# A graph network kernel: one merged pass for the second graph's rows, and expert tiles gathered by slot lists instead of scattered

## What is computed

```python
x = x + _L0_ffn_ref(_layernorm(x)[None], ...)[0]      # softmax over 64 slices in 8 heads, attention between slices,
                                                      # out_x @ W_out + b_out
x = x + _L1_gnn_ref(_layernorm(x), W_u, b_u, W_v, src, dst)   # per edge: s_u = xn @ W_u.T + b_u, s_v = xn @ W_v.T
# _L1_ffn_ref: a mixture of 8 experts
logits = xt @ Wr + br; probs = softmax(logits)
top_p, top_idx = top_k(probs, 2); weights = top_p / top_p.sum()
xe = layernorm(xt) * ln_g[e] + ln_b[e]
y = gelu(xe @ W1[e] + b1[e]) @ W2[e] + b2[e]
out = sum over the 2 chosen experts of weight * y
```

## Time and profile before

| | us |
|---|---|
| median of 3 runs | 5433.22 (5426.08 to 5433.31) |
| the profiled execution, its own time | 5424.74 |
| its span on the core | 5422.7 |
| mean granted TensorE clock | 0.793 of full |

### The profile page before, as it was taken

One profiled execution on the slowest core, in us unless ns is written; L12 is line 12 of the kernel. 1 busy time (PEld: TensorE's weight loads), 2 busy tenths in 40 slices (PEclk: granted clock), 3 DMA queues, 4 the chain that ended last, 5 costly groups with the idle time before them and its releaser, 6 DMA issues. The chain is left out here.

```text
span 5422.7 us, 84287 instructions
## 1 busy us (share of the span) xinstructions
PE 3370.2 (62%) x13516; PEld 2423.1 (45%) x13517; DVE 2164.5 (40%) x4578; ACT 1770.5 (33%) x6845; POOL 2313.1 (43%) x2387
## 2 busy tenths in 40 slices
PE   4401766666777766598844555545455550599998
PEld 3200443343444444365723333333333340599998
DVE  4401655555656555785523333333233332011111
ACT  2100333333333333242323233333333353344443
POOL 5151545454555555100455555555555535222222
PEclk9855888888888888798767777777777755799999
DMA  8441332233332323320133333333333332566665
GB/s 200 119 120 42 81 74 77 73 75 75 79 79 76 77 75 77 79 62 2 42 80 80 87 80 82 81 82 80 78 83 83 79 110 75 144 181 181 177 181 147
DMA packets 321085, 509.24 MB, mean 94 GB/s; under 512 B 153801, under 2 KB 222442, under 8 KB 320534
## 3 DMA queue, kind: packets, MB, share of 16 engines
q0 software_dynamic: 127744, 324.85, 24.3%
q1 hardware_dynamic: 180523, 179.06, 11.5%
q10 hardware_dynamic: 12770, 4.81, 0.4%
HBM read 429.99 MB, written 79.01 MB: 94 GB/s over the span
## 5 line engine op out<-in xcount | busy, mean ns | idle before, releaser
L822 POOL DMA_INDIRECT g_rows<-rows,g_recs x1856 | 1757.1, 947 | 1700.5 <-DVE g_msg L978 1001.9
L863 PE MATMUL g_pA<-g_msg,k_ident 128*128 128x264 f32 x3712 | 1157.4, 466 | 426.4 <-DVE g_msg L978 350.6
L863 PEld LDWEIGHTS g_pA<-g_msg,k_ident 128*128 128x128 f32 x3712 | 836.7, 236 | 784.6 <-issue 626.7
L978 DVE TENSOR_TENSOR g_msg<-g_rows,g_pp 128x1024 f32 (+1 forms) x464 | 565.4, 1218 | 1224.9 <-ACT g_pp L919 1116.3
L936 ACT ACTIVATE g_accs<-g_pA,g_cs x2928 | 709.5, 304 | 1047.8 <-issue 697.2
L851 PE MATMUL g_pE<-g_ew,g_recT 128*128 128x512 f32 x936 | 617.1, 795 | 424.8 <-ACT g_recT L897 401.4
L865 PE MATMUL g_pA<-g_accs,k_ident 128*128 128x264 f32 x928 | 347.0, 460 | 459.5 <-ACT g_accs L936 350.3
L851 PEld LDWEIGHTS g_pE<-g_ew,g_recT 128*128 128x128 f32 x936 | 211.2, 241 | 652.2 <-issue 631.0
L865 PEld LDWEIGHTS g_pA<-g_accs,k_ident 128*128 128x128 f32 x928 | 197.9, 226 | 546.1 <-ACT g_accs L936 379.7
L1926 POOL DMA_INDIRECT out<-e_ys,e_goal x102 | 157.1, 1540 | 600.6 <-issue 564.8
L1961 PE MATMUL e_pH<-e_xT,e_w 128*128 128x128 f32 x3264 | 384.6, 276 | 0.0
(11 more groups left out here) (394 smaller groups left out, 3521.9 us busy)
## 6 DMA issues: line engine op xcount, KB each, us to landing
e_w<-in_L_ffn_W SPq DMA_DIRECT2D x110, 1024.0 KB
g_rows<-rows,g_recs POOLq DMA_INDIRECT x1856
xs<-f_zero SPq DMA_DIRECT2D x1, 13674.0 KB
e_xs<-xs SPq DMA_DIRECT2D x102, 128.0 KB
g_recs<-slots SPq DMA_DIRECT2D x468, 8.0 KB
rows<-p_row SPq DMA_DIRECT2D x50, 119.0 KB
own<-p_row SPq DMA_DIRECT2D x50, 119.0 KB
p_x<-in_x SPq DMA_DIRECT2D x1, 5600.0 KB
```

The source lines that it names most:

```text
L822: pool.indirect_dma_start(out=rows[:, r, j, :], out_offset=None, in_=rows_d, in_offset=bass.IndirectOffsetOnAxis(ap=recs[:, r, 4 * j:4 * j ...
L863: t_.matmul(pA[:, b, 0:MW], K["ident"][:], msg[:, b, j, :], start=(j == 0), stop=False)
L978: v.tensor_tensor(to, of, by, ALU.mult).then_inc(msg_ok, 1)
```

## The change

**The second graph's rows.** f3 becomes one pass, written out without loops. In slot p TensorE multiplies tile p by `mm`, straight from `swT` (no copies on GpSimd), into one of four PSUM tiles, transposes tile p - 10 and makes the scores of tile p - 11. VectorE adds the product to `x`, takes the statistics, every seventh slot computes mean and variance of the last seven tiles, and two slots later their scales. ScalarE writes the normalized tile directly into the row buffer, which has eight rows of tiles instead of six. The bias is no longer added tile by tile: in f2 one eighth of it is added to every row of `mm` (the slice weights of each of 8 heads sum to one).

**The expert tiles.** Instead of scattering each node's row twice, e0 writes the normalized rows once and in order to a new DRAM tensor `tok`, 7 DMAs of 7 tiles from SyncE, each row with its output row number and both weights; row 0 is the pad. The list of rows for each expert tile is made on the chip: a place in the list is split in its low 7 bits and the tile number; for each of 98 pairs of node tile and choice VectorE makes a one-hot matrix of the low bits (`at_lo`, 128x128) and one of the tile numbers (`at_hi`, 128x106) times a code, twice the row number in `tok` plus 0 or 1 for the choice, and TensorE accumulates all 98 products in one PSUM tile. Its column t is the list of tile t; a place that no node takes stays 0, the pad row. In e1 GpSimd loads a tile's rows by an indirect gather with column t of the list (`load`), where SyncE had a plain DMA. It issues `load` of tile t + 3 between the add of tile t - 1 and that of tile t. VectorE picks output row and weight of a tile from the gathered rows (`keep`), two tiles ahead. The zeroing of `xs` and the strided DMA of the row numbers go away. The diff, cut to its core:

```diff
 KC = HID // 128
-XW = D + 2
...
-            zero = m2.sb("f1_zero", [Q, XW])
-            zeroed = T("zeroed"); z_out = T("z_out")
...
-                    pool.memset(zero[:], 0.0).then_inc(zeroed, 1)
-                    pool.wait_ge(zeroed, 1)
-                    pool.iota(zero[:, D:D + 1], pattern=[[0, 1]], base=N, channel_multiplier=1, allow_small_or_imprecise_dtypes=True).then_inc(zeroed, 1)
...
-                    sp.wait_ge(zeroed, 2)
-                    sp.dma_start(dr["xs"].rearrange("(t p) c -> p t c", p=Q), over(zero[:], 1, MT)).then_inc(z_out, 16)
-                    sp.wait_ge(z_out, 16)
...
+                    sp.dma_start(bout[:], ins["L0_ffn_b_out"].unsqueeze(0).broadcast_to([128, D])).then_inc(b_in, 16)
...
+                    dve.wait_ge(b_in, 16)
+                    ch.link(v.tensor_scalar(bout[:], bout[:], 1.0 / FH, None, ALU.mult))
...
-                    v.tensor_copy(mm[:].rearrange("p (a b) c -> p a (b c)", a=2), pM[:])
+                    v.tensor_tensor(mm[:].rearrange("p (a b) c -> p a b c", a=2), pM[:].rearrange("p a (b c) -> p a b c", b=2),
+                                    over(over(bout[:], 1, 2), 1, 2), ALU.add)
...
+            RB, PB, GT, LAG = 8, 4, 7, 10
...
+                    def product(t):
+                        if t >= PB:
+                            pe.wait_ge(y_used, t - PB + 1)
                         for k in range(4):
-                            last = t_.matmul(pY[b][:], swb[:, b, k, :], mm[:, k, :], start=(k == 0), stop=(k == 3))
+                            last = t_.matmul(pY[t % PB][:, 0:D], swT[:, k, t, :], mm[:, k, :], start=(k == 0), stop=(k == 3))
                         last.then_inc(y_ok, 1)
...
+                    def turn(t):
                         pe.wait_ge(xn_ok, t + 1)
+                        if t >= 2:
+                            pe.wait_ge(xnT_ok, t - 1)
                         for k in range(2):
-                            last = t_.transpose(pT[b][:, k, 0:Q], xn[:, b, k * 128:(k + 1) * 128], K["ident"][0:Q, 0:Q])
+                            last = t_.transpose(pT[t % 2][:, k, 0:Q], row[:, t % RB, k * 128:(k + 1) * 128], K["ident"][:])
                         last.then_inc(t_ok, 1)
...
+                    for p in range(QT + LAG + 1):
+                        if p < QT:
+                            product(p)
+                        if p == LAG:
+                            pe.wait_ge(w_in, 48)
+                        if 0 <= p - LAG < QT:
+                            turn(p - LAG)
+                        if 0 <= p - LAG - 1 < QT:
+                            scores(p - LAG - 1)
...
+                    def root(g):
+                        ts = slice(g * GT, (g + 1) * GT)
+                        act.wait_ge(stats, g + 1)
+                        s.activation(norm.rstd[:, ts], norm.rstd[:, ts], ACT.Sqrt).then_inc(sq, 1)
+                    def normed(t):
+                        act.wait_ge(rst, t // GT + 1)
+                        if t >= RB:
+                            act.wait_ge(row_out[t % RB], 16 * (t // RB))
+                        s.activation(row[:, t % RB, 0:D], x1[:, t, :], ACT.Identity, bias=norm.nbias[:, t:t + 1],
+                                     scale=norm.rstd[:, t:t + 1]).then_inc(xn_ok, 1)
...
+                    root(0)
+                    for t in range(QT + 1):
+                        if t < QT:
+                            if t % GT == GT - 2 and t // GT + 1 < ng:
+                                root(t // GT + 1)
+                            normed(t)
+                        if t >= 1:
+                            turned(t - 1)
...
+                    def update(t):
                         dve.wait_ge(y_ok, t + 1)
-                        dve.sem_inc(pace, 1)
-                        ch.link(v.tensor_tensor(xt, xt, pY[b][:], ALU.add))
...
+                        v.tensor_tensor(x1[:, t, :], x1[:, t, :], pY[t % PB][:, 0:D], ALU.add).then_inc(y_used, 1)
+                        dve.wait_ge(y_used, t + 1)
+                        norm.tile(v, t, x1[:, t:t + 1, :]).then_inc(tile_ok, 1)
...
+                    def ready(t):
+                        dve.wait_ge(u_ok, t + 1)
+                        v.tensor_copy(K["sdst"][:, t, :], pU[t % 2][:, H:2 * H])
+                        v.tensor_tensor(row[:, t % RB, D:RW], pU[t % 2][:, 0:2 * H], bu[:], ALU.add).then_inc(row_ok, 1)
+                    for p in range(last_slot):
+                        g = (p - GT - 2) // GT
+                        if p >= GT + 2 and (p - GT - 2) % GT == 0 and g < ng:
+                            dve.wait_ge(sq, g + 1)
+                            norm.scales(v, ch, rst, slice(g * GT, (g + 1) * GT))
+                        if p < QT:
+                            update(p)
+                            if p % GT == GT - 1:
+                                dve.wait_ge(tile_ok, p + 1)
+                                norm.variance(v, ch, stats, slice(p - GT + 1, p + 1))
+                        if p == LAG:
+                            dve.wait_ge(w_in, 48)
+                        if 0 <= p - LAG - 1 < QT:
+                            ready(p - LAG - 1)
...
+            xall = m2.sb("e0_xall", [Q, QT, XW])
+            xt = xall[:, :, 0:D]
+            xrow = m2.sb("e0_xrow", [Q, 2, D])
...
+                    sp.wait_ge(pad_ok, 2)
+                    sp.dma_start(dr["tok"][0:1, :], pad[:]).then_inc(tok_out, 16)
+                    sp.wait_ge(meta_ok, 1)
+                    kept = dr["tok"][1:1 + NPAD, :].rearrange("(t q) c -> q t c", q=Q)
+                    for g in range(QT // GT):
+                        sp.wait_ge(row_ok, GT * (g + 1))
+                        sp.dma_start(kept[:, g * GT:(g + 1) * GT, :], xall[:, g * GT:(g + 1) * GT, :]).then_inc(tok_out, 16)
+                    sp.wait_ge(tok_out, 16 * (QT // GT + 1))
...
+                    for t in range(QT):
+                        q = QL if t == QT - 1 else Q
+                        for k in range(2):
+                            s = 2 * t + k
+                            pe.wait_ge(at_ok, s + 1)
+                            t_.matmul(pL[:, 0:MT], at_lo[0:q, s % B, :], at_hi[0:q, s % B, :], start=(s == 0), stop=(s == 2 * QT - 1)).then_inc(listed, 1)
...
-                    def row(u, r, first):
...
-                            act.wait_ge(sent[r], 32 * u)
-                            act.sem_inc(pace, 1)
-                        for k in range(2):
-                            last = s.activation(xrow[:, r, k, 0:D], flat(xt[:, tc, :]), ACT.Identity, bias=norm2.nbias[:, tc],
-                                                scale=norm2.rstd[:, tc])
-                        last.then_inc(row_ok, 1)
...
+                    for t in range(QT):
+                        s.activation(xall[:, t, 0:D], xall[:, t, 0:D], ACT.Identity, bias=norm2.nbias[:, t:t + 1],
+                                     scale=norm2.rstd[:, t:t + 1]).then_inc(row_ok, 1)
...
+                        ch.link(v.tensor_scalar(lo_i[:], pos[k][:], Q - 1, None, ALU.bitwise_and))
+                        ch.link(v.tensor_copy(lo[k][:], lo_i[:]))
+                        ch.link(v.tensor_scalar(pos[k][:], pos[k][:], 7, None, ALU.arith_shift_right))
+                        ch.link(v.tensor_copy(hi[k][:], pos[k][:]))
+                    for t in range(QT):
+                        for k in range(2):
+                            s = 2 * t + k
+                            if s >= B:
+                                dve.wait_ge(listed, s - B + 1)
+                            v.tensor_scalar(at_lo[:, s % B, :], iota_q[:], lo[k][:, t:t + 1], None, ALU.is_equal)
+                            v.tensor_scalar(at_hi[:, s % B, :], iota_q[:, 0:MT], hi[k][:, t:t + 1], code[k][:, t:t + 1], ALU.is_equal, ALU.mult).then_inc(at_ok, 1)
...
+                    dve.wait_ge(listed, 2 * QT)
+                    ch.link(v.tensor_copy(code_i[:], pL[:, 0:MT]))
+                    v.tensor_scalar(lst[:], code_i[:], 1, None, ALU.arith_shift_right)
+                    ch.link(v.tensor_scalar(second_i[:], code_i[:], 1, None, ALU.bitwise_and))
+                    ch.link(v.tensor_copy(second[:], second_i[:]))
+                    ch.link(v.tensor_scalar(first_of[:], second[:], -1.0, 1.0, ALU.mult, ALU.add))
...
-                    def scatter(u, r, q):
-                        pool.wait_ge(idx_ok, u * R + (r + 1))
-                        pool.sem_inc(pace, 1)
-                        pool.wait_ge(row_ok, u * R + (r + 1))
-                        pool.sem_inc(pace, 1)
-                        for k in range(2):
-                            pool.indirect_dma_start(out=dr["xs"], out_offset=bass.IndirectOffsetOnAxis(ap=idx[r][k][0:q, 0:1], axis=0),
-                                                    in_=xrow[0:q, r, k, :], in_offset=None).then_inc(sent[r], 16)
...
-                    def load(u, b):
```

(45 more changed lines are left out.)

257 lines of the change are left out of this document (80 added, 177 removed).

## The result

The changed kernel takes 5571.14 us, median of 6 runs (5564.57 to 5573.47); the kernel before, 5429.55 over 6 runs (5419.95 to 5433.31). The ratio is 1.0261, 95% interval 1.0248 to 1.0274: 142 us slower, where 80 us faster was forecast. The profiled execution took 5570.72 us, with a span of 5569.0.

The account below looks back on a forecast made before the run. TensorE was taken to bound the expert tiles (busy 744 of 762 us), while scatters before them left it idle. 5424.7 - 44 - 89 - 6 + 55 = 5341, plus 8.5 for the median: 5350 us, range 5275 to 5430.

Parts of the forecast that it names:

- Merged pass: f3: one pass in TensorE-bound slots of 2.43 us, ending at 2680; gain 44 us, bounds 35 and 50.
- Rival C: f3: the merged pass falls to the half clock, 241 us instead of 132; 5459 us in all; chance 7%.
- Lists: Between routing and expert tiles: 98 one-hot pairs of 0.46 us replace the scatters; gain 89 us, bounds 74 and 104.
- Rival D: One-hot list loop: 1 us a pair if every VectorE-TensorE handshake shows; 53 us more, 5403 us; chance 8%.
- Start: Start of the expert tiles: most of TensorE's 5.76 us wait at tile 2 goes; gain 6 us, bounds 0 and 9.
- Gather in the steady stage: Expert tiles: gather late by 1.1 us, each step 0.55 longer; 99 steps cost 55 us, bounds 15 and 150.
- the ring: Expert tiles: gather of tile t + 3 hangs on tile t - 1's result; two steps a turn, 14.5 + 1.1 us.
- rival B: Expert tiles: gather waits behind a whole W1 load, late by 5.0 us, step 2.5 longer; 5543 us; chance 10%.

Follow-up runs that it names:

- the version whose tiles wait for nothing: Changed kernel with VectorE's small copies moved earlier and the gather of tile t+4 issued ahead of the add of tile t: 4151.8 us.
- no add: Changed kernel with expert rows written to the output without the accumulating add: 4382.7 us.
- half of W1: Changed kernel loading only the first half of W1's columns for all tiles after the first two: 4327.9 us.
- filler: Changed kernel with 10 extra 128x128 identity products on TensorE before the wait for gathered rows of every even tile from tile 4 on: 4391.1 us.

## Why the prediction was wrong, by its own steps

**Merged pass (44 us).** Right in all its parts: slots of 2.40 us for 2.43, clock 0.93 over the stretch, end at 2680.39 + 1.57 = 2682 for 2680, 42 us. On the other chips 35, since the old pass is shorter there. Rival C did not come.

**Lists (89 us).** The loop was right: 42.9 us (4457.4 to 4500.3) for 45; and the block that follows stands at 4505.0, where the working gives 4548.5 - 43.1 = 4505.4. That VectorE sets the pace (0.44) and not TensorE (0.46) was missed and made no difference. The gain was 102, because the old end was mis-sized: I let the expert tiles begin 1.9 us after the last scatter, at 4638, while the row of the next block in the earlier trace rows says 4650.48, 14.5 us after that scatter's end. What fills those 14.5 us is not shown: the DMA engines move nothing from 4642 on. Rival D did not come.

**Start (6 us).** The first activation comes 2.9 us later after its block (9.0 against 6.1: the first gather lands in 5.5 us, behind two W1 loads), and the wait at tile 2 is gone. The runs with and without it, 734.9 and 724.5 us, give 10.4, all in the first steps, since later both take 7.25 us a step: net 7.5.

**Gather in the steady stage (55 us).** Its working holds where no weights are in front: copy and semaphores from the add's end to the gather's start 1.0 us (1.2 taken with the gap), landing 2.06 (1.86). With W1 moved behind, the stage is 67 us longer than before; since that includes the faster start, the ring itself costs 77 for 55, 1.5 us a pair for 1.1. The step that failed is another: the landing was priced with nothing in front of the gather, 1.86 us, and it was 5.1, because 1 MB of W1 stood in front. That was the choice between this case and rival B. I set B at 10% with the sentence that "the weights of a step start about when the gather is nearly done". That was not read from a row. In the trace of the kernel before, in the very step of the earlier trace rows:

```profile
4996.74 0.38 SPq L1897 DMA_DIRECT2D e_w<-in_L_ffn_W  x1
```

By my own sum the gather would start at 4995.97 + 1.2 = 4997.2. The load goes out 0.4 us ahead of it, in this step as in its neighbours. With that row B had to be a likely case. I also took the Trainium skill's rule as a comfort, by which the gather "would wait for one packet of weights, not for a whole load"; it is none where a packet may be the whole load.

**Rival B (5543 us)** is what happened, at 5571. It priced a wait of 5.0 us for every pair, 1.1 of the ring and 3.9 of the load; the turn shown has 3.64 of idleness before the rows, 0.6 of other gaps, and 1.7 in slower products, together 6.0 for 20.5 - 14.5. That B came so near is in part luck: the load's share was 3.1 (5.13 - 2.08), not 3.9, and the clock's share was in no case of mine. On the other chips the changed kernel's 1018.7 us are 294 over the 724.5 of the version whose tiles wait for nothing: 77 of the ring, some 75 of the clock (an estimate, 47 falls of 1.6 each), and the rest, some 142, waiting behind W1.

The books, first chip, spans: blocks before the routing -45.1 (42 of it the merged pass), routing and lists -100.4, expert tiles +291.8; sum +146.3, which is 5569.0 - 5422.7.

## What to carry to other kernels

Where a change puts a small transfer on the ring that sets the pace, find in the trace of before which large transfer is issued near its place, and count the whole of that as in front of it, also when the small one would begin its issue a little sooner. About a microsecond in issue order decides. Two remedies are shown here, and neither is bandwidth: order (the small transfer issued to its end first, or the large one made to wait for it), and slack (the small one issued so early that it may land late). And once the busiest engine idles, price the clock it will have afterwards.

## What the hardware showed that I had not expected

- A 130 KB read issued 0.22 us behind a 1 MB load on another queue landed in 5.2 us, behind half of it in 3.7, behind none in 2.06, gathered or plain alike. With its issue (1.0 us) begun 0.40 us before the load it still took 4.8; with 1.12 us, 2.5 or less in all but a few turns.
- TensorE's granted clock fell to 0.50 for some 3 us after every one of 48 waits of 2.95 to 4.98 us in the changed kernel (47 of 48 on the other chips), after 30 of 48 waits of 2.8 to 3.4 us (no add), 14 of 48 of 1.8 to 3.0 (half of W1), 13 of 48 of 0.7 to 2.2 (filler), 2 of 48 with W1 loaded once and none with W1 behind the gather (both up to 2.1, mostly 0.8). Falls are counted by the 32 products behind the wait, 5 us or more instead of 3.8.
- GpSimd's copy of one column takes 0.75 us behind an accumulating scatter, 0.22 behind one that doesn't accumulate, and 0.18 where nothing is in front.
- The kernel before took 5430 us where the result was measured and 4280 to 4284 on the chips of the experiments (mean granted clock 0.793 and 0.872 over the span), with expert stages that agree to 1 us. The one pass compared differs at the same granted clock; the cause is open.
